# Two-layer graph transformer: the next group's norm transposes moved ahead of the down product, PSUM banks dealt anew, output norm later on VectorE

## What is computed

```python
# layer 0, 8 heads of 32, mask and edge bias from adj
nx = ln(x, ln1_g, ln1_b)
q, k, v = nx @ wq + bq, nx @ wk + bk, nx @ wv + bv
p = softmax(q @ k.T / sqrt(32) + where(adj > 0, 0.1 * adj * adj, -inf))
x1 = x + (p @ v) @ wo + bo
x2 = x1 + gelu(ln(x1, ln2_g, ln2_b) @ w1 + b1) @ w2 + b2
# layer 1, one head of 256, masked by adj
w = softmax(where(adj == 0, -inf, (x2 @ Wq) @ (x2 @ Wk).T / 16))
out = ln(x2 + (w @ (x2 @ Wv)) @ Wo + bo, gamma, beta)
```

## Time and profile before

| | before |
|---|---|
| median of 3 runs | 935.13 us (934.89 to 935.47) |
| profiled execution | 935.03 us, its span 933.3 us |
| granted TensorE clock | 0.993 (mean of the span) |
| TensorE matmul, weight load busy | 903.3 us, 805.8 us |
| VectorE, ScalarE, GpSimd busy | 691.0, 641.2, 388.6 us |

### The profile page before, as it was taken

One profiled execution on the slowest core, in us unless ns is written; L12 is line 12 of the kernel. 1 busy time (PEld: TensorE's weight loads), 2 busy tenths in 40 slices (PEclk: granted clock), 3 DMA queues, 4 the chain that ended last, 5 costly groups with the idle time before them and its releaser, 6 DMA issues.

```text
span 933.3 us, 22588 instructions
## 1 busy us (share of the span) xinstructions
PE 903.3 (97%) x7623; PEld 805.8 (86%) x7623; DVE 691.0 (74%) x2576; ACT 641.2 (69%) x1888; POOL 388.6 (42%) x257
## 2 busy tenths in 40 slices
PE   8889999999999999999999999999999999998995
PEld 8677798988889898888989888898988889898894
DVE  7676877869587786958779595877968687786745
ACT  5675958668496766858677585866758586685751
POOL 3425153543616354262535526263451626344221
PEclk9999999999999999999999999999999999999998
DMA  7101000010101001010100101010010100000001
GB/s 260 35 1 35 2 24 24 30 29 0 56 0 34 22 22 34 0 51 6 34 22 22 34 0 35 22 34 22 22 34 0 34 22 28 11 24 1 24 1 34
DMA packets 29727, 26.29 MB, mean 28 GB/s; under 512 B 1126, under 2 KB 29436, under 8 KB 29692
## 3 DMA queue, kind: packets, MB, share of 16 engines
q1 hardware_dynamic: 29676, 25.83, 8.8%
q10 hardware_dynamic: 16, 0.00, 0.0%
HBM read 17.44 MB, written 8.39 MB: 28 GB/s over the span
## 4 chain that ended last, share of the span: by engine, by line
PE 43%; issue 21%; DVE 15%; POOL 14%; ACT 6%; POOLq 1%; DVEq 0%; ACTq 0%
PE bank L327 10%; PE bank L329 9%; PE bank L328 9%; DVE nx L1083 4%; POOL x L1519 4%; DVE hT_lo L1009 3%; PE bank L471 3%; POOL y L1524 3%; PE bank L564 3%; PE bank L592 3%; ACT bank L829 2%; PE bank L463 2%; POOL adj_s L1468 2%; POOL bias L1477 2%; POOL rstd L1450 2%
## 5 line engine op out<-in xcount | busy, mean ns | idle before, releaser
L804 ACT ACTIVATE bank<-p_s,neg_max 128x128 f32<-128x128 f32 x512 | 182.2, 356 | 24.1 <-DVE neg_max L1112 23.9
L1450 POOL TENSOR_TENSOR rstd<-ve,minus_half 128x4 f32<-128x4 f32 (+1 forms) x51 | 54.9, 1077 | 312.8 <-DVE ve L1076 312.8
L327 PE MATMUL bank<-w_hi,hT_hi 128*128 128x256 f32 x512 | 147.4, 288 | 0.0
L329 PE MATMUL bank<-w_hi,hT_lo 128*128 128x256 f32 x512 | 144.1, 282 | 0.0
L328 PE MATMUL bank<-w_lo,hT_hi 128*128 128x256 f32 x512 | 144.1, 281 | 0.0
L1112 DVE CUSTOM_DVE_ANT_0 p_s<-bank,bias 128x128 f32<-128x128 f32 x512 | 112.5, 285 | 8.4 <-PE bank L463 8.3
L327 PE MATMUL bank<-n2T_hi,w_hi 128*128 128x512 f32 (+1 forms) x272 | 110.1, 405 | 3.4 <-DVE qk_lo L1010 3.3
L829 ACT ACTIVATE bank<-bank,vec_cols 128x512 f32<-128x512 f32 (+1 forms) x136 | 86.6, 637 | 30.5 <-PE bank L329 30.5
L329 PE MATMUL bank<-n2T_hi,w_lo 128*128 128x512 f32 (+1 forms) x272 | 104.0, 382 | 0.0
L328 PE MATMUL bank<-n2T_lo,w_hi 128*128 128x512 f32 (+1 forms) x272 | 103.8, 382 | 0.0
L327 PEld LDWEIGHTS bank<-w_hi,hT_hi 128*128 128x128 f32 x512 | 96.4, 188 | 2.5 <-DVE hT_lo L1009 0.8
(11 more groups left out here) (211 smaller groups left out, 2460.4 us busy)
## 6 DMA issues: line engine op xcount, KB each, us to landing
xs<-in_x SPq DMA_DIRECT2D x15, 512.0 KB, 3.7
out<-y SPq DMA_DIRECT2D x15, 512.0 KB, 2.9
adj_i<-in_adj SPq DMA_DIRECT2D x15, 256.0 KB, 2.8
x2T_f<-in_L_gnn_w SPq DMA_DIRECT2D x1, 512.0 KB, 7.0
tT<-in_L_gnn_w SPq DMA_DIRECT2D x1, 512.0 KB, 7.8
y<-in_L_gnn_w SPq DMA_DIRECT2D x1, 512.0 KB, 6.4
vo<-in_L_gnn_w SPq DMA_DIRECT2D x1, 512.0 KB, 7.8
x_bo<-in_x SPq DMA_DIRECT2D x1, 256.0 KB, 2.8
```

Source lines behind the costliest of these rows:

```text
L327: mm(out, a_hi, b_hi, start=first, stop=False)
L329: return mm(out, a_lo, b_hi, start=False, stop=last)
L804: last = run(bank[r][:, NODES * place:NODES * place + NODES], p_s[:, r, place, :], ACT.Exp, scale=-1.0, bias=neg_max[:, r, place:place + 1 ...
L1450: P.tensor_tensor(t["rstd"][:, 0:k], t["ve"][:, 0:k], minus_half[:, 0:k], ALU.pow).then_inc(ln_pool[n], 1)
```

## The change

- **TensorE.** `norm_transpose(gp)` moves from between the two halves of the down product to right behind `scores(ga, 1)`; the two halves follow each other. The transposes now use banks 4 and 5 (6 and 7 for groups 0 and 1), the down halves banks 6 and 7.
- **Waits that follow from the banks.** `norm_transpose(gp, gb)` waits for six `h_low` of `gb`; `mlp_down(gb, 0)` for seven in place of five, except for the very last group; `project_v(gp, 0)` for the first `residual2(gb)`. The second product of the layer 1 weights, once in the first turn, goes to bank 7 and waits for eight `h_low`, and the first `x2_transpose` for its low part.
- **VectorE.** `moments(1, gp)` moves up to right behind `sums1(gp)`; `norm1(gp)` and `h_low(gb, 4)` to ahead of `residual1(ga, 0)`; `norm3(gc)` from ahead of `residual1(ga, 0)` to ahead of `attn_low(ga, 1)`. The last turn keeps its order.
- **GpSimd.** `gain` and `offset` move behind `bias(gp)`; `x2_plus_bo` behind `rstd(2, ga)`.

```diff
-        down_bank = (4, 5)
-        nx_bank, k_bank, q_bank, v_bank = (6, 7), (5, 6), (5, 4), (6, 5)
+        down_bank = (6, 7)
+        nx_bank, k_bank, q_bank, v_bank = (4, 5), (5, 6), (5, 4), (6, 5)
...
-        l1_bank, l1_mm_bank = (5, 4, 5), (7, 5)
+        l1_bank, l1_mm_bank = (5, 4, 5), (7, 7)
...
         def at(n, g):
+            if n == "nx":
+                return (6, 7) if isinstance(g, int) and g < 2 else nx_bank
...
# l1_product
-                    pe.wait_ge(dve_h, 6)
+                    pe.wait_ge(dve_h, 8)
...
-            def norm_transpose(g):
+            def norm_transpose(g, gb=None):
+                if gb is not None:
+                    pe.wait_ge(dve_h, HT * gb + 6)
...
# mlp_down
                 if q == 0:
-                    pe.wait_ge(dve_h, HT * g + 5)
+                    pe.wait_ge(dve_h, HT * g + (5 if is_last(g) else 7))
...
# x2_transpose
+                if isinstance(g, int) and g == 0:
+                    pe.wait_ge(dve_lo, SPLIT["vo1"])
...
# turn, TensorE
                 if A2:
                     scores(ga, 1)
+                if P:
+                    norm_transpose(gp, gb)
                 if first:
                     l1_product(1)
                     pe.wait_ge(dve_lo, SPLIT["w2"])
                 mlp_down(gb, 0)
-                if P:
-                    norm_transpose(gp)
                 if B and size(gb) > 2:
                     mlp_down(gb, 1)
                 if A2:
                     p_transpose(ga, 1)
                 if P:
+                    if B:
+                        pe.wait_ge(dve_x2, pair0(gb) + 1)
                     project_v(gp, 0)
...
# turn, VectorE
                     sums1(gp)
+                    moments(1, gp)
                 if A:
                     attn_low(ga, 0)
                 if B:
                     h_low(gb, 3)
                 if P:
-                    moments(1, gp)
-                if C:
-                    norm3(gc)
+                    norm1(gp)
+                if B:
+                    h_low(gb, 4)
                 if A:
                     residual1(ga, 0, B)
                 if B:
-                    for j in range(4, HT):
+                    for j in range(5, HT):
                         h_low(gb, j)
                 if A2:
                     biased(ga, 1, 0)
-                if P:
-                    norm1(gp)
...
                     pT_copy(ga, 1, 3)
+                if C:
+                    norm3(gc)
+                if A2:
                     attn_low(ga, 1)
...
# turn, GpSimd
+                if P:
+                    adjacency(gp)
+                    edges(gp)
+                    bias(gp)
                 if C:
                     gain(gc, size(gc))
                     offset(gc, size(gc))
-                if P:
-                    adjacency(gp)
-                    edges(gp)
-                    bias(gp)
-                if B:
-                    x2_plus_bo(gb)
                 if A and B:
                     rstd(2, ga)
                     pool.wait_ge(ln_dve[2], ln_end(ga))
+                if B:
+                    x2_plus_bo(gb)
```

More of the change, by code:

```diff
@@ L412, in norm_transpose @@
                     for b in range(size(g)):
-                        last = tr(bank[nx_bank[t]][:, nodes(b)], nx[:, b, 128 * t:128 * t + 128], ident[:, :])
+                        last = tr(bank[at("nx", g)[t]][:, nodes(b)], nx[:, b, 128 * t:128 * t + 128], ident[:, :])
                     last.then_inc(pe_nxT, 1)
@@ L781, in nxT_copy @@
                     act.wait_ge(pe_nxT, 2 * g + t + 1)
-                    identity(nxT[0][:, t, toks(g)], bank[nx_bank[t]][:, toks(g)]).then_inc(act_nxT, 1)
+                    identity(nxT[0][:, t, toks(g)], bank[at("nx", g)[t]][:, toks(g)]).then_inc(act_nxT, 1)
             def k_copy(g, t):
@@ L1103, in nxT_low @@
                     dve.wait_ge(act_nxT, 2 * g + t + 1)
-                    low(nxT[1][:, t, toks(g)], bank[nx_bank[t]][:, toks(g)], nxT[0][:, t, toks(g)]).then_inc(dve_nxT, 1)
+                    low(nxT[1][:, t, toks(g)], bank[at("nx", g)[t]][:, toks(g)], nxT[0][:, t, toks(g)]).then_inc(dve_nxT, 1)
             def biased(g, q, r):
@@ L1537, in turn @@
                     pool.wait_ge(ln_dve[1], ln_end(gp))
-                if C:
-                    gain(gc, size(gc))
-                    offset(gc, size(gc))
                 if P:
@@ L1544, in turn @@
                     bias(gp)
-                if B:
-                    x2_plus_bo(gb)
+                if C:
+                    gain(gc, size(gc))
+                    offset(gc, size(gc))
                 if A and B:
```

## The result

The changed kernel takes 940.91 us (median of four runs: 940.33, 940.35, 941.48, 941.84), the kernel before, run beside it, 935.18 us (934.89 to 935.47). The ratio is 1.0062, 95% interval 1.0045 to 1.0080: slower by more than the 0.2% that can be told. Predicted were 941.0 us and a range of 937.3 to 943.8. The profiled execution took 941.84 us, its span 940.1.

What follows compares the result with a forecast made beforehand. TensorE's own rate was taken to bound the kernel. Steady turns 2.2, turns around the loop 0.05, first turn 1.7 and last 1.9 sum to 5.9 us over 935.03: 940.9, said as 941.0, range 937.3 to 943.8.

Steps and rivals of the forecast that it cites:

- Part 1: Down product in one piece on TensorE: one re-entry less, gain 0.05 us per turn, bounds 0 and 0.10.
- Part 2: VectorE's new order ahead of `residual1`: second scores 0.23 us later per steady turn, bounds 0.13 and 0.49.
- the upper bound of part 2: Scores 0.49 us later per steady turn, if `rstd(1)` takes 1.30 us and not 1.04.
- `rstd(1)`: GpSimd's step ahead of `norm1`: 1.04 us assumed; the rival had 1.30, giving 944.1 us, chance 0.10.
- Part 3: New waits of a steady turn for `h_low` and `residual2`: nothing won or lost.
- Part 4: Later `norm3`, `gain` and `offset`: cost 0, 1.5 us of idle left before `rstd(2)`, `tT` wait still 0.28.
- Part 5: First turn: scores 0.83 us late plus transposes 0.87 on the path, cost 1.7 us, bounds 0.9 and 2.3.
- Part 6: Last turn: group 15's down product waits for seven `h_low`, starting 2.47 us late, net cost 1.9 us.
- `residual1` earlier: Rival: `residual1` earlier, not later, ending 0.4 us of idle weight load at the scores: 932.8 us, chance 0.04.
- The wait for `tT`: Rival: this wait goes as `x2_plus_bo` no longer precedes `rstd(2)`, 4.9 us off: 936.0 us, chance 0.05.
- First and last turn: Rival: these two turns don't pay for the change: 937.3 us, chance 0.07.
- `gain` and `offset`: Rival: on GpSimd they hold up `rstd(2)`, so `norm2`, `tT` and the query projection: 947 us, chance 0.05.

Runs made afterwards that it cites:

- e9: Changed kernel with the norm transposes between the two down halves again in every turn, all else as changed: 942.44 us, ratio 1.0060.
- e4: Changed kernel with `h_low(4)` back behind `residual1` on VectorE in every turn: 941.24 us, ratio 1.0058.
- e8: Kernel before with only the output norm's part: `norm3`, `gain` and `offset` later, `x2_plus_bo` behind `rstd(2)`: 936.41 us, ratio 0.9997.
- e2: Changed kernel, in the first turn alone the norm transposes stand between the down halves again: 941.86 us, ratio 1.0062.
- e5: Changed kernel with group 15's old down banks and wait, the first turn's old TensorE and VectorE order, and `h_low(4)` behind `residual1`: 936.33 us, ratio 0.9986.
- e1: Changed kernel, group 15's down product in the last turn back on banks 4 and 5, waiting for five `h_low`: 940.43 us, ratio 1.0045.
- e7: e5 with VectorE's `t_copy(gb)` ahead of `norm2(ga)`: 929.03 us, ratio 0.9916.
- e3: e2 with `norm1` also back behind the biased scores in the first turn, `moments(1)` staying ahead of `attn_low`: 941.16 us, ratio 1.0056.
- e6: Changed kernel with VectorE's `t_copy(gb)` ahead of `norm2(ga)`: 935.93 us, ratio 0.9984.
- e10: Kernel before with only VectorE's `t_copy(gb)` moved ahead of `norm2(ga)`, nothing of the change: 928.74 us, ratio 0.9912.

## Why the prediction was right, point by point

- **Part 1, the undivided down product:** 0.05 us per turn predicted, 0.07 measured in the turn shown (13.49 to 13.42), 0.055 in the mean of twelve, 0.05 by e9.
- **Part 2, VectorE ahead of `residual1`:** right step by step. Predicted from the start of `sums1`: `norm1` at 3.39 us (440.40 - 437.01), scores at 6.02 (443.03 - 437.01). Measured: 444.46 - 441.07 = 3.39 and 447.09 - 441.07 = 6.02. By the same steps the scores are 443.03 - 442.83 = 0.20 late; 0.19 was measured in this turn, 0.18 in the mean. I had taken 0.23, for an `attn_low` that might be up to 0.08 later; this 0.05 too much is nearly all of the miss per turn, 0.136 net in place of 0.18, and 1.6 in the loop in place of 2.2. e4 shows that `h_low(4)` decides: without it the lateness vanishes. Two bounds were wrong: without the pause for `rstd` (0.13) the lateness would be 0.07 to 0.10, not 0.13, and with the upper bound of part 2 the time is 944.1, outside the range that was said to hold it.
- **`rstd(1)`** took 1.01 us beside `attn_low` and `h_low`, so 1.04 was the right row and 1.30 fell. The Trainium skill, "SBUF — State Buffer", section "Who interferes with whom", has a VectorE instruction with one SBUF input outside the two-port modes leave GpSimd alone; this row agrees. The prediction's other use of that section went too far: the port pair is taken for one instruction, not for four in a row, so it does not say that `rstd` waits for all of `norm3`. Before's trace has 1.30 or 1.31 us for `rstd` beside four `norm3` instructions, 1.16 beside two (at 111.46, in the second turn) and 1.04 beside none: 0.06 to 0.07 us for each.
- **Part 3, the new waits of a steady turn:** 0 predicted, 0 measured. In after the transposes wait for an `h_low` that ends at 446.96 + 0.68 = 447.64, 0.55 us ahead of them, and the down product for one that ends at about 448.3, 0.7 ahead. e9 shows that the cover is the transposes.
- **Part 4, output norm, `gain`, `offset`:** 0 predicted. `rstd(2)` keeps 1.73 us of idle (1.5 predicted), the wait for `tT` is unchanged at 0.28, and e8 costs nothing. The turns around the loop came to 0.02 - 0.12 = -0.10 in place of +0.05; in the one behind the loop the down product and the four transposes take 11.89 us in place of 12.00, so there the undivided product gives 0.11 and not 0.05.
- **Part 5, the first turn:** 1.7 predicted, 1.75 measured, `project_v` at 77.7 once the start-up is taken off. The terms are 0.79 for the scores (0.83 predicted) and 0.82 for the transposes (0.87). The other 0.14 is in neither term: `p_transpose` of this turn is 0.10 longer than before also in e2 and e5, and which part of the change does that no run tells. The sum is right, in part by luck, for one step was not named: I charged all the lateness of the scores to `norm1`. Nearly half of it is `moments(1)` (0.37 us: the two up products ahead of the output projection and their waits take 2.26 us, in before and in e5 1.90), and 0.50 is `norm1`, less 0.08 by which this execution was ahead before them. `moments(1)` does not fit into the shorter pause of this turn, 0.27 us before `attn_low` in place of 0.65 in a steady one, and delays the projection. My step for `attn_low` was checked in the steady turn alone. I had also priced nothing for `l1_product`'s wait for eight `h_low`; it lies hidden in after and shows as soon as the rest is undone.
- **Part 6, the last turn:** 1.9 predicted, 1.91 measured; idle of 2.47 predicted, 2.45 measured. e1 settles it.
- **The sum:** 5.9 predicted, 5.2 by the segments, 5.15 between the two faster runs of after and the median of before. That the median came within 0.1 us of 941.0 is partly luck: two of the four runs were over 1 us slower, most likely by a longer start-up, which lifts it by 0.6.
- **The rivals:** `residual1` earlier fell with the measured 0.19 late, and by e8 its price of 0.4 us per turn was wrong too (14 x 0.4 is 5.6, moreover, and not 5.3). The wait for `tT` did not go. First and last turn paid 3.7 us. `gain` and `offset` did not hold up `rstd(2)`.

## What to carry to other kernels

When the engine that sets the time and the one that feeds it arrive together, an instruction is not free because as long a one was taken away: count the chain from its last fixed point, with its pauses for other engines. Price a new wait in each turn where it applies, the odd ones at the ends above all; here two of sixteen turns made two thirds of the loss, and the one wait of a bank dealt anew made half of that. And the gain was elsewhere: a copy that needed only TensorE stood behind a norm that waited for a third engine, and exchanging the two was worth more than the whole reordering.

## What the runs showed of the hardware

**The start-up goes with the granted clock.** Windows of the trace from 5 to 35 us; columns: busy time of PE, PEld, DVE, ACT, POOL with the number of instructions, granted TensorE clock, DMA share, GB/s. Before, after and e7:

```profile
5.00:35.00 30.00, 26.70 (x235) 23.87 (x234) 22.89 (x86) 20.63 (x59) 14.13 (x15) 0.94 0.57 188
```

```profile
5.00:35.00 30.00, 27.12 (x232) 25.09 (x232) 21.66 (x82) 19.80 (x57) 14.20 (x14) 0.89 0.59 188
```

```profile
5.00:35.00 30.00, 27.32 (x219) 25.85 (x219) 20.98 (x79) 17.02 (x54) 14.10 (x14) 0.77 0.58 188
10.00:15.00 5.00, 5.00 (x25) 5.00 (x24) 4.41 (x15) 1.53 (x4) 2.86 (x5) 0.50 0.95 334
```

The order up to there is the same in all kernels, but the clock is not, and the twelve traces fall into three groups by it. With 0.94 the first up product comes at 45.99 to 46.42 us (before, e3, e6, e9, e10), with 0.89 at 47.76 to 48.56 (after, e1, e2, e4, e5), with 0.77 at 50.54 and 50.55 (e8, e7). A clock of 0.50 is TensorE at 1.2 in place of 2.4 GHz: from 10 to 15 us e7 starts 25 of its matmuls, e10 59. The times of the kernel before spread in the same way: beside e1 to e4, five of eleven runs lie at 934.9 to 935.6 and six at 936.9 to 937.4, and beside e5 to e8 four of 27 at 938.9 to 941.4, up to the time of the changed kernel. Those runs have no trace. What decides the clock in a given execution no run here tells.

**A wait of 2.45 us can cost more than itself.** In e2, whose last turn is after's, TensorE comes out of the same wait at half rate:

```profile
886.81 0.58 PE L329 MATMUL bank<-w_hi,hT_hi 128*128 128x256 f32 x1 [2.45 <-DVE hT_lo L1019]
...
887.83 0.41 PE L330 MATMUL bank<-w_lo,hT_hi 128*128 128x256 f32 x1
888.05 0.41 PE L331 MATMUL bank<-w_hi,hT_lo 128*128 128x256 f32 x1
```

Its window from 887 to 889 us, in the columns named above:

```profile
887.00:889.00 2.00, 2.00 (x10) 2.00 (x11) 0.57 (x2) 0.00 (x0) 1.63 (x2) 0.50 0.05 17
```

A product every 0.21 us for 3 us, where after has one every 0.12 at a clock of 1.00. The profiled executions of e2, e3 and e4 all have it, at slightly different places, and their last turns are 81.98 to 82.19 us in place of 80.67; e1, without the wait, has 78.78. After, e6 and e9 have the wait and not the slow stretch, and none of the six kernels without the wait has such a stretch at that place. e4 and e6 had another such stretch in the first turn, behind three short waits of `p_transpose` and one at `project_v` (1.16, 0.16, 0.15 and 0.49 us in e4), and with it e4's first turn is 0.87 us longer than after's, which has nearly the same waits and a clock of 1.00. So in the profiled executions of e2, e3 and e4 the slow stretch takes back what the segment before it gained, and this is most likely why their medians show no gain; the other runs have no trace. What makes one execution drop its clock there and another not, these runs do not tell.
